# A delta-rule attention, two expert mixtures and a decay attention on one core: redrawn instruction orders, and a few pieces of work given to another engine

## The reference, cut to what matters

```python
x = x + attn_a(norm(x))   # 8 heads; convolved q, k, v; gated delta rule
x = x + ffn(norm(x))      # 15 experts, 3 picked, and a shared one
x = x + attn_b(norm(x))   # decay attention
x = x + ffn(norm(x))
# attn_a, one head, one token; nh = 3 keys and values a token
S = S * exp(g)
for i in range(3):
    S = S + beta_i * k_i (v_i - k_i^T S)
o = q^T S                  # q and k are divided by their lengths, q by sqrt(128) too
o = o * rsqrt(mean(o*o) + 1e-5) * rms_weight * silu(x @ Wg);  y = concat(o) @ Wo
# attn_b, for each token
state = (1 - w) * state + k v^T;   out = r^T state;   y = out @ Wo
```

## Time and profile before

| | us |
|---|---|
| median of 3 runs | 3138.93 |
| the profiled execution, its own time | 3139.86 |
| its span in the trace | 3138.0 |
| busy in the span: PE | 2919.0 (93%) |
| DVE | 2486.9 (79%) |
| ACT | 2346.9 (75%) |
| POOL | 1977.9 (63%) |
| 0 to 72.5 us: prologue | 72.5 |
| 72.5 to 2300 us: the frames, filling and draining included | 2227.5 |
| 2680 to 2870 us: decay attention | 190 |

### The profile page before, as it was taken

One profiled execution on the slowest core, in us unless ns is written; L12 is line 12 of the kernel. 1 busy time (PEld: TensorE's weight loads), 2 busy tenths in 40 slices (PEclk: granted clock), 3 DMA queues, 4 the chain that ended last, 5 costly groups with the idle time before them and its releaser, 6 DMA issues. The chain is left out here.

```text
span 3138.0 us, 84065 instructions
## 1 busy us (share of the span) xinstructions
PE 2919.0 (93%) x27212; PEld 2241.5 (71%) x27212; DVE 2486.9 (79%) x5731; ACT 2346.9 (75%) x7723; POOL 1977.9 (63%) x3127
## 2 busy tenths in 40 slices
PE   5569999999999999999999999999987999768999
PEld 3448888888888888888888888888776444455444
DVE  5669999999999999999999999999754455594544
ACT  4769999999999999999999999999754443314443
POOL 1588888888888888888888888888831000100000
PEclk8779999999999999999999999999998999868999
DMA  5457777777777777777777777777532323002242
GB/s 108 123 147 179 190 187 180 180 184 174 184 187 191 182 182 182 178 179 182 193 184 182 183 179 182 180 189 181 154 96 75 152 102 152 10 3 78 107 160 115
DMA packets 588208, 482.91 MB, mean 154 GB/s; under 512 B 464784, under 2 KB 504368, under 8 KB 581632
## 3 DMA queue, kind: packets, MB, share of 16 engines
q1 hardware_dynamic: 579328, 474.39, 57.4%
q10 hardware_dynamic: 8448, 3.15, 0.4%
HBM read 285.53 MB, written 191.86 MB: 152 GB/s over the span
## 5 line engine op out<-in xcount | busy, mean ns | idle before, releaser
L953 DVE SCALAR_TENSOR_TENSOR conv_k<-PP,tk,conv_k 128x256 f32<-128x256 f32 x1536 | 718.5, 479 | 101.0 <-ACT conv_k L772 75.7
L953 DVE SCALAR_TENSOR_TENSOR conv_v<-PP,tv,conv_v 128x256 f32<-128x256 f32 x1152 | 540.5, 478 | 57.4 <-ACT conv_v L772 43.1
L710 POOL TENSOR_TENSOR X<-X,tmp 96x31 f32<-96x31 f32 (+15 forms) x992 | 534.3, 539 | 77.8
L707 POOL TENSOR_TENSOR tmp<-At,X 96x31 f32<-96x31 f32 (+15 forms) x992 | 486.7, 491 | 63.3 <-DMA At<-n_d 5.1
L1114 PE MATMUL PP<-xn,wk 128*128 128x268 f32 x1024 | 342.5, 418 | 41.4 <-DVE conv_k L953 29.7
L675 POOL TENSOR_TENSOR Sg<-S,gend 128x512 f32<-128x512 f32 x256 | 266.6, 1041 | 63.3 <-DVE S L912 63.3
L744 ACT ACTIVATE recA<-TG,es 96x128 f32<-96x128 f32 x1024 | 285.0, 367 | 6.3 <-DVE es L946 6.3
L693 POOL TENSOR_TENSOR rk<-ss,half 96x8 f32<-96x8 f32 x128 | 209.0, 1633 | 125.9 <-DVE ss L921 119.6
L1078 PE MATMUL RB<-rhs,Yf 96*96 96x128 f32 x2048 | 269.7, 274 | 18.7 <-DVE rhs L901 18.4
L772 ACT ACTIVATE conv_k<-PP,tk 128x256 f32<-128x256 f32 x512 | 245.2, 480 | 46.6 <-PE PP L1114 26.1
L1068 PE MATMUL RA<-S,kqgB 128*96 128x128 f32 x2048 | 276.1, 278 | 1.0 <-DVE S L912 1.0
(11 more groups left out here) (292 smaller groups left out, 6578.4 us busy)
## 6 DMA issues: line engine op xcount, KB each, us to landing
kqg_d<-kqgA SPq DMA_DIRECT2D x128, 512.0 KB, 6.4
kqgB<-kqg_d SPq DMA_DIRECT2D x128, 512.0 KB, 4.4
rec_d<-recA SPq DMA_DIRECT2D x128, 480.0 KB, 3.4
recB<-rec_d SPq DMA_DIRECT2D x128, 480.0 KB, 6.1
f1gates<-f1gates_d SPq DMA_DIRECT2D x24, 1024.0 KB, 6.8
f2gates<-f2gates_d SPq DMA_DIRECT2D x24, 1024.0 KB, 6.9
gdec<-gdec_d SPq DMA_DIRECT2D x128, 128.0 KB, 5.8
apk_d<-apkA SPq DMA_DIRECT2D x128, 128.0 KB, 3.3
```

What stands on the lines that cost most here:

```text
L707: nc.gpsimd.tensor_tensor(t, At[q % 2][:, j, j + 1:].unsqueeze(2).broadcast_to(sh), X[q % 2][:, j, 0:cols].unsqueeze(1).broadcast_to(sh), ...
L710: nc.gpsimd.tensor_tensor(x, x, t, ALU.subtract).then_inc(sub_ev, 1)
L953: return nc.vector.scalar_tensor_tensor(acc, src[:, :, j:j + SPAN], w[:, j:j + 1], acc, ALU.mult, ALU.add)
```

## The change

The parts that are more than an order:

1. Prologue: of the eight decay tables VectorE clears the even ones, GpSimd the odd ones. Only head 0's table is sent to DRAM in the prologue. The tables of heads 1 to 7 are sent by SP in the frame loop, four DMAs in each of seven passes.
2. The gate product of the queries (128x256) goes from GpSimd (L661) to a new VectorE stage `qg_`.
3. The four ScalarE copies of `q2_` become four DMAs of SP (`q2_copy`, 32 partitions of two numbers each). The constant goes into `mo_` and the norm weight. `ss` gets two buffers.
4. `m3` multiplies with 32 columns of `Zt`.
5. Both `mo_` stand together behind the second `o_`.
6. Decay attention: level 6 goes by `far` instead of a mask; the products of k in `merge` go from VectorE to GpSimd (`keys`); 11 instead of 6 pairs (l, b) stand between the tiles.

The orders of all five queues in the frame loop are drawn anew, and the loop is one pass longer (the names shift by one frame, c - 1 for c and so on; SP's `at_load`, `da_load` and `dec_load` and GpSimd's first `sg` keep their f and so stand a pass earlier against the rest).

```diff
@@ prologue
-            for h in range(NH):
-                sp.wait_ge(mask_ev, h + 1)
-                for b in range(B - 1):
-                    keep_table(sp, h, b)
+            sp.wait_ge(mask_ev, 1)
+            for b in range(B - 1):
+                g.keep_table(sp, 0, b)
...
+            for h in range(1, NH, 2):
+                pool.wait_ge(ex_ev, h + 1)
+                x = ex[:, h, :].rearrange("p (c t) -> p c t", t=TC)
+                nc.gpsimd.tensor_tensor(x, x, upto, ALU.mult).then_inc(odd_ev, 1)
@@ delta_attention
+            def tables(h):
+                if 0 < h < NH:
+                    for b in range(B):
+                        keep_table(sp, h, b)
+            def q2_copy(N):
+                if not live(N):
+                    return
+                need(sp, ss_ev, N)
+                need(sp, fo_ev, N - RING)
+                for b in range(B):
+                    sp.dma_start(q2[TC * b:TC * (b + 1), N % RING, :], ss[N % 2][R:128, NCC * b:NCC * (b + 1)]).then_inc(st_q2[N % 2], 16)
...
-                at_load(*group_at(f, GROUP + 1))
-                x_store(*group_at(f, 2 * GROUP + 1))
-                rec_load(c)
-                da_load(c + 1)
-                weights(*divmod(f, KSTEPS))
-                dec_load(f)
-                kqg_store(f - 1)
-                rec_store(f - 1)
-                ap_store(f - 1)
-                y_load(c + 1)
+                rec_load(c - 1)
+                y_load(c)
+                ap_store(f - 2)
+                x_store(*group_at(f - 1, 2 * GROUP + 1))
+                kqg_store(f - 2)
+                weights(*divmod(f - 1, KSTEPS))
+                tables(f - 1)
+                at_load(*group_at(f, GROUP + 1))
+                da_load(c + 1)
+                rec_store(f - 2)
+                q2_copy(f - 2)
+                dec_load(f)
...
-                nc.gpsimd.tensor_tensor(kqgA[N % 2][:, :, R:128], kq[N % 2][:, :, R:128], d, ALU.mult).then_inc(kqg_ev, 1)
...
+            def qg_(N):
+                if not live(N):
+                    return
+                need(dve, qsilu_ev, N)
+                dve.wait_ge(ld_dec[N % 2], 2 * uses(N))
+                if N >= 2:
+                    dve.wait_ge(st_kqg[N % 2], uses(N - 2))
+                d = gdec[N % 2][:, :, :].rearrange("p b (c t) -> p (b c) t", t=TC)
+                nc.vector.tensor_tensor(kqgA[N % 2][:, :, R:128], kq[N % 2][:, :, R:128], d, ALU.mult).then_inc(qg_ev, 1)
@@ decay_attention
-    MASKED, W = 7, 64
+    MASKED, W = 6, 64
...
+            def keys(l, b):
+                if not l:
+                    return
+                pool.wait_ge(up_ev, ups[l - 1, b] + 1)
+                pool.wait_ge(p_mm, products(l, b) + 1)
+                k = halves(kB, l, b)[:, :, 0, :]
+                nc.gpsimd.tensor_tensor(k, k, last_of_half(l, b, 1), ALU.mult).then_inc(kup_ev, 1)
...
-                nc.vector.tensor_tensor(kv[:, :, 0, :], kv[:, :, 0, :], end, ALU.mult)
-                nc.vector.tensor_tensor(rv[:, :, 1, :], rv[:, :, 1, :], mid, ALU.mult).then_inc(t_ev, 1)
-                dve.wait_ge(t_ev, ups[l, b] - len([x for x in ups if x[0] == 0 and ups[x] < ups[l, b]]) + 1)
-                nc.vector.tensor_tensor(fv[:, :, 1, :], fv[:, :, 1, :], mid, ALU.mult).then_inc(up_ev, 1)
+                r, f, mid = halves(rF, l, b)[:, :, 1, :], halves(F, l, b)[:, :, 1, :], last_of_half(l, b, 0)
+                nc.vector.tensor_tensor(r, r, mid, ALU.mult)
+                dve.wait_ge(kup_ev, kups[l, b] + 1)
+                nc.vector.tensor_tensor(f, f, mid, ALU.mult).then_inc(up_ev, 1)
```

More of the change, by code:

```diff
@@ new lines, in _ @@
+                sup(r - 1, 0)
+                tap1(f - 1, "k0")
+                qg_(f - 2)
+                tap2(f - 1, "k0")
+                tap1(f - 1, "k1")
+                tap3(f - 1, "k0")
+                rhs_(r - 1, 1)
+                ap(f - 2, 1)
+                tap2(f - 1, "k1")
+                tap3(f - 1, "k1")
+                tap1(f - 1, "k2")
+                vr(c - 1, 1)
+                ap(f - 2, 0)
+                tap2(f - 1, "k2")
+                tap1(f - 1, "q")
+                tap3(f - 1, "k2")
@@ L1094, in o_ @@
                 need(pe, wev_ev[cc], N)
-                if cc:
-                    need(pe, mo_ev[0], N)
-                else:
+                if not cc:
                     need(pe, acc_ev, N - 1)
@@ L1658, in decay_attention @@
         NP = NEAR + len(FAR)
-        pair_of = lambda n: 3 if n < 2 * B else n % 4
+        WITHIN = [[], [], [(0, 0)], [(1, 0), (2, 0)], [(0, 1), (3, 0)], [(1, 1), (4, 0)], [(0, 2), (2, 1)], [(1, 2), (3, 1)]]
+        TIGHT = sum(len(w) for w in WITHIN)
+        pair_of = lambda n: 3 if n < TIGHT else n % 4
         before = {n: max((m for m in range(n) if pair_of(m) == pair_of(n)), default=None) for n in range(NP)}
@@ L1675, in steps @@
                 yield "tile", i
-                for l in range(2):
-                    b, odd = divmod(i - 2 - l, 2)
-                    if not odd and 0 <= b < B - 1:
-                        yield "near", (l, b)
-            yield "near", (0, B - 1)
-            yield "near", (1, B - 1)
-            for l in range(2, LV + 1):
+                for x in WITHIN[i]:
+                    yield "near", x
+            done = [x for w in WITHIN for x in w]
+            for l in range(LV + 1):
                 for b in range(B):
-                    yield ("near" if l < MASKED else "far"), (l, b)
+                    if (l, b) not in done:
+                        yield ("near" if l < MASKED else "far"), (l, b)
         order = [x for kind, x in steps() if kind == "near"]
         near_no = {x: n for n, x in enumerate(order)}
-        ups = {}
+        ups, kups = {}, {}
         for kind, x in steps():
@@ L1691, in decay_attention, with halves, last_of_half, products @@
                 ups[x] = len(ups)
+                if x[0]:
+                    kups[x] = len(kups)
+        def halves(t, l, b):
+            return t[:, b * T:(b + 1) * T].rearrange("p (n two h) -> p n two h", two=2, h=1 << (l - 1))
+        def last_of_half(l, b, right):
+            hs = 1 << (l - 1)
+            return halves(F, l, b)[:, :, right, hs - 1:hs].broadcast_to([128, T // (2 * hs), hs])
+        def products(l, b):
+            return near_no[l, b] if l < MASKED else far_no[l, b]
         @block.tensor
@@ L1880, in _ @@
                 spread(b)
-            for b in range(B):
-                far(LV, b)
+            for l, b in FAR:
+                far(l, b)
             for q in range(NG // 4):
```

278 lines of the change are left out of this document (132 added, 146 removed).

## The result

| | before | after |
|---|---|---|
| median of the runs, us | 3139.14 (4) | 3262.85 (4) |
| ratio, 95% interval | | 1.0386 (1.0359 to 1.0412) |
| span of the profiled execution, us | 3138.0 | 3261.7 |

The numbers in brackets are how many runs a median is of. The change is 3.9% slower. 3095 was forecast, with 3131 as the upper end. The rival on the right side, (c), was priced at 3167 and had a chance of 0.1.

The account below looks back on a forecast made before the run. VectorE was taken to bound three frames of four, ScalarE the fourth. From 3139.86: prologue -6, filling +3, frames -26, decay attention -15, sum -44, 3095.9, as median 3095; own range 3080 to 3110, wider range 3058 to 3131.

Parts of the forecast that it names:

- (c): Rival: SP's queue becomes the bound, groups of four frames slip 2.5 us each; +72, 3167 us; chance 0.1.
- SP in a frame: SP's queue in the frame loop: four more copies and landing waits make the state's loads late but within spare; cost none.
- SP's work: SP's issues per frame: 11.4 us now, four copies at 0.5 to 0.7 make 13.4 to 14.2 of 17.0.
- the sign: What would show the forecast right: among others, SP still waiting 3 us a frame.
- Frames, VectorE: Frame loop: queries' product +0.57, tap order -0.36, 0.6 of waits kept; mean frame 17.03 from 17.25, -26 us over 116 frames.
- 16.9 for frames one to three: Frame loop: VectorE bounds the first three frames of a group at 16.9 us; the fourth, where ScalarE turns, takes 17.4.
- Prologue and filling: Before the steady frames: loop starts earlier, -6 us (4.5 to 7.5); table stores in the filling cost +3 (0 to 10).
- Decay attention: Last stretch: VectorE's pairs get 0.73 us shorter at levels 1 to 5, level 6 loses its copy; -15 us (-25 to +5).
- (b): Rival: GpSimd's k products lock VectorE out in decay attention, 20 pairs, +21, 3116 us; chance 0.1.

Follow-up runs that it names:

- edit 6: Changed kernel with gdec's load reading 128 rows of its own instead of one shared row (decays wrong numbers): 3095.15 us, 0.9852 of the kernel before.
- edit 8: Kernel before with the state's loads moved behind the tables' loads: 3148.46 us, 1.0022 of the kernel before.
- edit 1: Changed kernel with the four q copies back on ScalarE instead of SP: 3130.88 us, 0.9979 of the kernel before.
- edit 3: Changed kernel with the state's loads (kqgB, recB) ahead of q's copies and the tables' loads on SP's queue: 3098.84 us, 0.9879 of the kernel before.
- edit 4: Changed kernel with the state's loads behind q's copies and ahead of the tables' loads: 3096.46 us, 0.9858 of the kernel before.
- edits 3 to 6: edit 3, edit 4, edit 6, and the changed kernel with the state's loads between the edec and gdec loads: 3093.72 us, 0.9848 of the kernel before.
- edit 10: Kernel before with only the change's new prologue, tables in the loop and new decay attention: 3123.91 us, 0.9942 of the kernel before.

## Why the prediction was wrong, step by step

- **The failing step is "SP in a frame".** It said that the state's loads "come late by about 0.9", "land after 6.1" and "have some 4.6 us to spare", cost none. The 6.1 (recB's; kqgB's was 4.4) came from rows of before, where these loads stood ahead of the tables' loads. The change puts them right behind, and there kqgB lands in 8.2 and recB in 9.1. The prediction counted what SP issues and forgot what a load stands behind. Priced by the runs: 3262.9 - 3095.2 = 168 us, from edit 6. The loss takes both halves, the late landing and SP's fuller pass: edit 8 has the first alone and loses 7 us, edit 6 has the copies on SP without the first and loses nothing, and edit 1 takes away the copies alone and brings 132 us back. An estimate from the rows: 0.9 late and 8.2 - 4.4 = 3.8 of landing use up the 4.6 us, and the issues that got longer go beyond.
- **SP's work** was sized well in itself. Four copies take 2.9 us in the changed kernel and 2.4 in edit 3, where 2.0 to 2.8 were put, and with gdec out of the way 2.5 to 3.4 us a frame are left where 3 were named as the sign. The longest pass was put at 17.8. The one shown above takes 19.1, with issues longer than in edit 6.
- **Rival (c)** had the side and the sign (TensorE waiting for kqgB at `ks`), and its growth of the landings by 2 us is about what came, 6.1 to 8.2 and 9.1. But it put that down to load, and it comes from gdec's load ahead: edit 4 keeps all of SP's issues and loses nothing. Its mechanism, too many issues on SP's queue, is half of the cause (edit 1). Priced at 2.5 us a group, it cost 5.4 ((18.61 - 17.25) x 4). Its chance of 0.1 was too low for a case in which two things that each fit must fit together.
- **Frames, VectorE.** Forecast 17.03, and with the queue mended 17.17 to 17.19 (edits 3 to 6). The queries' product was right: +0.57 forecast, and 0.51 from its start to the next (edit 3). `ss_` was missed: +0.41. The prediction asked only what two SBUF inputs do, for `qg_`, `es` and the products of decay attention; `ss_` has one. Where the new order puts the shortest instructions beside GpSimd was not asked. This term was -26 in the sum; 0.06 x 116 = 7 is what came.
- **The mean hides two more errors that partly cancel.** VectorE's busy time, in the mean of 100 frames, goes from 15.94 to 16.78 in edit 3, +0.84 where +0.21 was forecast, and its idle time from 1.31 to 0.39, where 0.6 of waits were kept. By frame it is not "16.9 for frames one to three" and 17.4 for the fourth, the turning one. In edit 3 the turning frame (the first here) is fast and the one behind it slow:

```profile
1005.88:1022.70 16.82, 16.29 (x180) 13.95 (x180) 16.02 (x40) 15.90 (x51) 12.97 (x27) 1.00 0.80 211
1022.70:1040.56 17.86, 17.32 (x183) 14.07 (x181) 17.52 (x40) 15.45 (x53) 16.63 (x26) 1.00 0.80 219
1040.56:1057.48 16.92, 16.64 (x180) 13.91 (x180) 16.64 (x40) 14.81 (x51) 14.25 (x20) 1.00 0.61 154
1057.48:1074.55 17.07, 16.56 (x181) 13.93 (x181) 16.89 (x40) 14.96 (x52) 13.98 (x23) 1.00 0.67 175
```

- **A gain not forecast** made up for part of it, in the draining of the frames: -19.1 us. The run of edit 10 keeps the old orders and has the old drain, so it belongs to the orders. That 3095 was met by edit 6 to the microsecond is therefore luck in part: in its trace the terms are -2 up to the first steady frame, -6 for the frames, -20 for the drain and -15 for decay attention, in place of -3, -26, nothing and -15.
- **Prologue and filling.** Forecast -6 and +3. The loop starts 4.3 us earlier (68.23 against 72.53), just outside the bounds of 4.5 to 7.5; the first `es` comes 3.6 us earlier (83.6 against 87.2) and the filling takes all of it back. GpSimd's mask took 2.3 to 2.7 us where 2.1 was put, and one of VectorE's beside it 1.85 instead of 1.22:

```profile
63.13 1.85 DVE L356 TENSOR_TENSOR ex<-ex,p_upto 128x1024 f32<-128x1024 f32 x1 [1.45 <-ACT ex L251]
...
64.89 2.34 POOL L272 TENSOR_TENSOR ex<-ex,p_upto 128x1024 f32<-128x1024 f32 x1 [0.99 <-ACT ex L251]
...
68.23 0.57 SPq L554 DMA_DIRECT2D edec<-edec_d  x1
```

- **Decay attention.** Forecast -15, measured -14.3. In the middle levels a pair takes 2.42 us (2918.03 - 2915.61), as worked out. Rival (b) happens where GpSimd's k comes beside r and F:

```profile
2915.61 0.68 DVE L2013 TENSOR_TENSOR b_F<-b_F 128x512 f32<-128x512 f32 x1
...
2917.43 0.69 DVE L2011 TENSOR_TENSOR b_rF<-b_rF,b_F 128x512 f32<-128x512 f32 x1
2918.03 0.69 DVE L2013 TENSOR_TENSOR b_F<-b_F 128x512 f32<-128x512 f32 x1
...
2920.29 4.54 POOL L1943 TENSOR_TENSOR b_kB<-b_kB,b_F 128x512 f32<-128x512 f32 x3 [0.43 <-PE b_pair L1792]
2922.30 1.53 DVE L2011 TENSOR_TENSOR b_rF<-b_rF,b_F 128x512 f32<-128x512 f32 x1
2923.76 1.63 DVE L2013 TENSOR_TENSOR b_F<-b_F 128x512 f32<-128x512 f32 x1
```

## What to carry to other kernels

When an order on a DMA queue changes, read each load's landing together with what stands ahead of it. A landing time taken from the old order belongs to the old neighbour. A load that all partitions read from one small piece of DRAM is best issued behind the loads that an engine waits for (edits 3 to 5). Spreading it over rows first took the delay away as well (edit 6), but what it costs to write such rows was not tried. A wait of TensorE for a load can also cost it clock, as the 19 falls above show. When instructions move on VectorE, ask for each of them, the shortest too, what GpSimd does at that moment.

## What the runs showed of the hardware that was not expected

- 128 KB read by 128 partitions from one shared 1 KB land in 5.2 us (one piece) or 6.6 (four pieces of 256 bytes, in the fuller queue of the changed kernel); from 128 rows of their own in 2.8 or 3.1. The DMA engines are nearly idle for over 2 us meanwhile (9 to 41 GB/s), and what is issued behind it on the same queue lands up to 4 us later (kqgB 8.2, and 4.3 behind own rows). Why is open.
- DMA issues on SP's queue are longer in the kernel that is held up: a small store n_d takes 0.93 us in the mean from 500 to 2000 us and 0.59 in edit 6, a load of Yf 0.71 and 0.45.
- A VectorE instruction of 0.16 us, with one SBUF input, is held until the GpSimd instruction beside it ends (66 of 88 in edit 3; the other 22 still longer): 0.80 us from its start to the next beside Sg. The record (1.33 in the mean there) is longer than the time for which the engine is held.
- TensorE's clock falls from 2.4 to 1.2 GHz 19 times in 1500 us of the changed kernel, at idle times of 1.6 to 4.8 us; in the kernel before, with none above 1.5, it never does.
